# Packing the edge messages of a graph layer by 128-edge blocks with a slot table, in a four-layer graph network

## The reference

```python
xs = x[:, :C] @ (W_in2f_s / np.sqrt(C))
xv = jnp.einsum('nci,cf->nfi', x[:, C:].reshape(n, C, 3), W_in2f_v) / np.sqrt(C)
sj = xs[idx_j]; vj = xv[idx_j]
...
h = shifted_softplus(f_ij @ Wf1 + bf1)
W = (h @ Wf2 + bf2) * rcut_ij[:, None]
...                                      # products of sj, vj, a direction Yv and W: one message per edge
agg = jax.ops.segment_sum(x_ij, idx_i, num_segments=n)
```

## Time and profile before

| | |
|---|---|
| Time, median of 3 runs | 2368.18 us (2367.39 to 2369.47) |
| Time of the profiled execution | 2369.56 us |
| Its span (first to last instruction) | 2367.9 us |
| Fourth layer's edge loop | 1324 to 2318 us of the span |
| PE busy | 2152.2 us (91%), 8194 matmul instructions |
| DVE busy | 1680.3 us (71%) |
| ACT / POOL busy | 1208.7 us (51%) / 1285.7 us (54%) |

### The profile page before, as it was taken

The page is one execution under the profiler, slowest core; times in us unless marked ns, Lnnn a source line. Parts: engine busy times, 40 slices in busy tenths (PEclk is TensorE's granted clock), DMA queues, the critical chain, the costliest instruction groups (busy, mean ns, idle before and its releaser), DMA issues.

```text
span 2367.9 us, 39830 instructions
## 1 busy us (share of the span) xinstructions
PE 2152.2 (91%) x8194; PEld 1246.1 (53%) x8194; DVE 1680.3 (71%) x4797; ACT 1208.7 (51%) x3485; POOL 1285.7 (54%) x1637
## 2 busy tenths in 40 slices
PE   3798976777779999999999899999999999999997
PEld 3444434666664555454444555555555555555555
DVE  7998798888882431102225688888888888888885
ACT  0486566777770000000101667667676767666764
POOL 1578856666666666560002566666666666666650
PEclk9698987666669999999999899999999999999998
DMA  5200031111012111210000433333333333333331
GB/s 192 72 3 3 3 106 16 14 15 15 14 15 61 33 37 15 50 19 1 23 19 5 127 94 101 97 99 98 99 99 99 99 95 102 95 103 94 101 94 44
DMA packets 72826, 146.45 MB, mean 62 GB/s; under 512 B 23565, under 2 KB 36098, under 8 KB 72391
## 3 DMA queue, kind: packets, MB, share of 16 engines
q0 software_dynamic: 46080, 103.42, 17.9%
q1 hardware_dynamic: 23740, 36.99, 4.7%
q10 hardware_dynamic: 2946, 5.28, 0.6%
HBM read 122.80 MB, written 22.30 MB: 61 GB/s over the span
## 4 chain that ended last, share of the span: by engine, by line
PE 76%; DVE 17%; issue 4%; DVEq 2%; DMA 1%; ACT 0%; POOL 0%; ACTq 0%; SPq 0%; POOLq 0%
PE ps L840 26%; PE ps L589 11%; PE ps L608 8%; PE ps L826 4%; PE ps L781 4%; PE ps L828 3%; PE ps L827 3%; PE ps L829 3%; PE ps L739 3%; PE ps L681 3%; DVE dense L1332 2%; DVE adj_t L1356 2%; DVE dense L1331 2%; DVE adj_t L1161 2%; PE ps L704 1%
## 5 line engine op out<-in xcount | busy, mean ns | idle before, releaser
L840 PE MATMUL ps<-adj_t 128*128 128x512 f32 x1408 | 671.4, 599 | 0.0
L484 POOL DMA_INDIRECT src_table<-st_rec,st_idx x320 | 386.5, 1208 | 271.7 <-DMA st_rec<-records 179.5
L1048 ACT ACTIVATE adj_t<-adj_t 128x128 f32<-128x128 f32 x1056 | 344.6, 389 | 218.5 <-DVE adj_t L1510 217.4
L531 POOL DMA_INDIRECT adj_t<-z_table,adj_t x352 | 339.1, 963 | 168.4 <-DVE adj_t L1520 79.8
L840 PEld LDWEIGHTS ps<-adj_t 128*128 128x128 f32 x1408 | 253.3, 189 | 256.6 <-issue 216.3
L472 POOL DMA_INDIRECT pair_table<-dense x160 | 197.7, 1236 | 112.7 <-issue 112.7
L739 PE MATMUL ps<-dense 128*128 128x128 f32 x832 | 243.0, 429 | 0.0
L826 PE MATMUL ps<-dense_r 128*128 128x512 f32 x352 | 217.7, 618 | 2.3 <-POOL dense_r L539 2.3
L608 PE MATMUL ps<-wring,dense 128*128 128x512 f32 (+1 forms) x480 | 208.6, 597 | 4.6 <-issue 3.2
L739 PEld LDWEIGHTS ps<-dense 128*128 128x128 f32 x832 | 200.5, 296 | 15.6
L539 POOL TENSOR_TENSOR dense_r<-adj_t,dense_r 128x512 fp32r<-128x512 f32 x88 | 113.6, 1291 | 169.0 <-ACT dense_r L1057 168.8
(11 more groups left out here) (248 smaller groups left out, 3787.1 us busy)
## 6 DMA issues: line engine op xcount, KB each, us to landing
src_table<-dense SPq DMA_DIRECT2D x8, 704.0 KB, 7.0
adj_t<-src_table SPq DMA_DIRECT2D x88, 64.0 KB, 1.8
adj_t<-z_table,adj_t POOLq DMA_INDIRECT x352, 3.5
src_table<-st_rec,st_idx POOLq DMA_INDIRECT x320, 2.6
records<-dense SPq DMA_DIRECT2D x1, 5000.0 KB
st_rec<-records POOLq DMA_DIRECT2D x80, 62.5 KB, 2.2
wring<-in_edge_attr SPq DMA_DIRECT2D x2, 1562.5 KB
wring<-in_l_w SPq DMA_DIRECT2D x3, 1024.0 KB, 7.5
```

The source lines that it names most:

```text
L484: g.indirect_dma_start(out=src_table, out_offset=bass.IndirectOffsetOnAxis(ap=st_idx[0:EP, k, c:c + 1].bitcast(u32), axis=0), in_=st_rec[0 ...
L531: g.indirect_dma_start(out=zg[:, s, c, :], out_offset=None, in_=z_table, in_offset=bass.IndirectOffsetOnAxis(ap=dsti[:, s, c:c + 1].bitcas ...
L840: last = mm(bank[6 + h], oh[:, c, :], msg[:, c, h * D:(h + 1) * D], start=c == 0, stop=c == GROUP - 1)
L1048: last = A(msg[:, c, (2 + k) * P:(3 + k) * P], msg[:, c, MSG:MSG + P], ACT.Copy, scale=side[:, s, c, C_Y - ATT + k:C_Y - ATT + k + 1])
```

## The change

Tiles are padded to whole chunks (128 edges) instead of whole groups. At most `USED` = 322 chunks are then used. A tile's chunks are dealt out as items of four, two or one chunks, and a tile can have at most one item of two and one of one. Fixed places are kept for the worst case: 73 items of four (`FOURS`), 10 of two, 10 of one. A group now holds one item of four, or two items of two, or four items of one, so there are 73 + 5 + 3 = 81 groups (the last has two chunks), together 322 chunks. Items that a tile does not need load an empty chunk of padding.

Where an item's chunks begin in `src_table` and which tile it sums into is computed on the chip: `item_table` (DVE, some 50 small operations, behind the row sums of the adjacency), two small matmuls on PE (a new stage `slots`, between `deg` and `l1a_agg`), and two copies on DVE into `src_at` and `src_offs`. `chunk_steps(SRC)` and `chunk_places(SRC)` of the preparation go.

SP loads an offset from `src_at` into a register before each load, and issues one load per item (one, two or four per group). Each item has its own accumulation on PE and its own `add_sums` on DVE. In groups of twos and ones (`alone`), the filters of the next group stand ahead of scatters 2 and 3 instead of behind them. The loop now runs over groups 2 to 69; groups 0, 1 and 70 to 80 are written out.

```diff
-QUANT_LOG2 = [7, 9]
-GROUPS = (E + NT * (GROUP * P - 1)) // (GROUP * P)
-GROUPS += GROUPS % 2
-SRC_CHUNKS = GROUPS * GROUP
+USED = (E + NT * (P - 1)) // P
+FOURS = math.ceil((USED - 3 * NT) / 4)
+LISTS = [(4, FOURS, 0), (2, NT, 80), (1, NT, 96)]
+EMPTY = USED
+SRC_CHUNKS = 8 * math.ceil((EMPTY + GROUP) / 8)
+GROUPS = FOURS + NT // 2 + math.ceil(NT / GROUP)
+def items_of(g):
+    if g < FOURS:
+        return [(g, 0, 4)]
+    if g < FOURS + NT // 2:
+        return [(LISTS[1][2] + 2 * (g - FOURS) + k, 2 * k, 2) for k in range(2)]
+    one = GROUP * (g - FOURS - NT // 2)
+    return [(LISTS[2][2] + one + k, k, 1) for k in range(min(GROUP, NT - one))]
+LOOP_TO = (FOURS - 2) // 2
...
-                sp_eng.dma_start(recg[:, s, :, :].rearrange("p c w -> p (c w)"),
-                                 tsrc[:, ds(g * (GROUP * SRC_COLS), GROUP * SRC_COLS)]).then_inc(rec_in[s], 16)
+                for slot, c, n in items_of(g) if isinstance(g, int) else [(g, 0, GROUP)]:
+                    at = sp_eng.value_load(src_at[0:1, ds(slot, 1)], min_val=0, max_val=EMPTY * SRC_COLS)
+                    sp_eng.dma_start(recg[:, s, c:c + n, :].rearrange("p c w -> p (c w)"),
+                                     tsrc[:, ds(at, n * SRC_COLS)]).then_inc(rec_in[s], 16)
...
+            b = bank_for("slots", 0)
+            pe.wait_ge(slots_ready, 1)
+            for k in range(2):
+                last = mm(b[0:1, k * P:(k + 1) * P], slots[:, k:k + 1], ident[:, :], start=True, stop=True)
...
-                if c == 0 and not (isinstance(i, int) and gi == 0):
-                    pe.wait_ge(agg_added, gi)
+                if c == c0 and not (isinstance(i, int) and gi == 0):
+                    pe.wait_ge(agg_added, items_before(gi) + k)
...
-                scatter(i, s, 2)
-                if one:
-                    filter_out(*nxt, 0)
-                scatter(i, s, 3)
-                if one:
-                    filter_out(*nxt, 1)
+                for c in range(2, count):
+                    if one and alone:
+                        filter_out(*nxt, c - 2)
+                    scatter(i, s, c)
+                    if one and not alone:
+                        filter_out(*nxt, c - 2)
...
+            def item_table():
+                for k, (size, count, at) in enumerate(LISTS):
+                    link(v.tensor_copy(left_i, left))
...
+                v.tensor_reduce(slots[:, 1:2], place_of, AX.X, ALU.add).then_inc(slots_ready, 1)
...
+                for c in range(chunks_of(g)):
+                    one_hot(i, s, c)
+                    messages(i, s, c, nxt=(i if s == 0 else i + 1, 1 - s) if c == 1 and not tail else None)
+                    if c == 0 and not head:
+                        add_sums(g - 1, len(items_of(g - 1)) - 1 if isinstance(g, int) else 0)
+                    if c in ends:
+                        add_sums(g, ends[c])
```

More of the change, by code:

```diff
@@ L45 @@
 BURST = 8
-FILL = 44
+FILL = SRC_CHUNKS // 8
 assert SRC_CHUNKS % FILL == 0
@@ L261, in build @@
         pos_read = [sem(f"pos_read{s}") for s in range(2)]
-        off_done = [sem(f"off_done{s}") for s in range(2)]
+        off_done = sem("off_done")
         rows_ready = [sem(f"rows_ready{s}") for s in range(2)]
-        offs_ready = [sem(f"offs_ready{s}") for s in range(2)]
+        offs_ready = sem("offs_ready")
+        slots_ready = sem("slots_ready")
         tick = sem("tick")
@@ L423, in _ @@
             sp_eng.wait_ge(full, first["l2_agg"] + NT)
+            sp_eng.wait_ge(done["slots"], 1)
             load_group(0, 0)
             load_group(0, 1)
-            with sp_eng.Fori(1, L3_IT) as i:
+            with sp_eng.Fori(1, LOOP_TO + 1) as i:
                 load_group(i, 0)
                 load_group(i, 1)
+            for g in range(2 * LOOP_TO + 2, GROUPS):
+                load_group(g // 2, g % 2)
         @block.gpsimd
@@ L546, in group @@
                 if one:
+                    count = chunks_of(2 * i + s + 1)
                     gather(*nxt, 0)
@@ L561, in _ @@
             group(0, 1)
-            with pool.Fori(1, L3_IT - 1) as i:
+            with pool.Fori(1, LOOP_TO) as i:
                 group(i, 0)
                 group(i, 1)
-            group(L3_IT - 1, 0, two=False)
-            group(L3_IT - 1, 1, one=False, two=False)
+            for k in range(2 * LOOP_TO, GROUPS):
+                group(k // 2, k % 2, one=k + 1 < GROUPS, two=k + 2 < GROUPS)
         @block.tensor
@@ L836, in scatter @@
                 pe.wait_ge(oh_ready, n + 1)
-                if c == 0 and not (isinstance(i, int) and gi == 0):
-                    pe.wait_ge(agg_added, gi)
+                items = items_of(gi) if isinstance(gi, int) else [(gi, 0, GROUP)]
+                k = [q for q, (_, c0, count) in enumerate(items) if c0 <= c < c0 + count][0]
+                _, c0, count = items[k]
+                if c == c0 and not (isinstance(i, int) and gi == 0):
+                    pe.wait_ge(agg_added, items_before(gi) + k)
                 for h in range(2):
-                    last = mm(bank[6 + h], oh[:, c, :], msg[:, c, h * D:(h + 1) * D], start=c == 0, stop=c == GROUP - 1)
+                    last = mm(bank[6 + h], oh[:, c, :], msg[:, c, h * D:(h + 1) * D], start=c == c0, stop=c == c0 + count - 1)
                 last.then_inc(scat_chunk, 1)
@@ L845, in group @@
                 nxt = (i, 1) if s == 0 else (i + 1, 0)
-                filter_out(i, s, 2)
+                count = chunks_of(2 * i + s)
+                alone = isinstance(i, int) and 2 * i + s >= FOURS
+                if count > 2:
+                    filter_out(i, s, 2)
                 scatter(i, s, 0)
@@ L869, in _ @@
             group(0, 1)
-            with pe.Fori(1, L3_IT - 1) as i:
+            with pe.Fori(1, LOOP_TO) as i:
                 group(i, 0)
                 group(i, 1)
-            group(L3_IT - 1, 0, two=False)
-            group(L3_IT - 1, 1, one=False, two=False)
-            pe.wait_ge(agg_added, GROUPS)
+            for g in range(2 * LOOP_TO, GROUPS):
+                group(g // 2, g % 2, one=g + 1 < GROUPS, two=g + 2 < GROUPS)
+            pe.wait_ge(agg_added, items_before(GROUPS))
             tbank = [(bank[0], bank[1]), (bank[4], bank[5])]
@@ L1083, in group @@
                     first_vy(*nxt, 0)
-                c_part(i, s, 3)
+                if count > 3:
+                    c_part(i, s, 3)
                 if two:
@@ L1099, in _ @@
             group(0, 1)
-            with act.Fori(1, L3_IT - 1) as i:
+            with act.Fori(1, LOOP_TO) as i:
                 group(i, 0)
                 group(i, 1)
-            group(L3_IT - 1, 0, two=False)
-            group(L3_IT - 1, 1, one=False, two=False)
+            for g in range(2 * LOOP_TO, GROUPS):
+                group(g // 2, g % 2, one=g + 1 < GROUPS, two=g + 2 < GROUPS)
             def sums(t):
@@ L1411, in _ @@
             dve.wait_ge(tiles_summed, 1)
+            item_table()
             dve.wait_ge(full, first["l0_agg"] + 12)
@@ L1422, in _ @@
             dve.wait_ge(done["deg"], 3)
+            b = taken("slots", 0)
+            link(v.tensor_scalar(src_at, b[0:1, 0:P], float(EMPTY * SRC_COLS), None, ALU.add))
+            v.tensor_copy(src_offs, b[0:1, P:2 * P]).then_inc(done["slots"], 1)
             scaled_T("l1a_agg")
@@ L1544, in _ @@
             group(0, 1)
-            with dve.Fori(1, L3_IT - 1) as i:
+            with dve.Fori(1, LOOP_TO) as i:
                 group(i, 0)
                 group(i, 1)
-            group(L3_IT - 1, 0)
-            group(L3_IT - 1, 1, tail=True)
-            add_sums(L3_IT - 1, 1)
+            for g in range(2 * LOOP_TO, GROUPS):
+                group(g // 2, g % 2, tail=g + 1 == GROUPS)
+            add_sums(GROUPS - 1, len(items_of(GROUPS - 1)) - 1)
             def activated(t):
```

129 lines of the change are left out of this document (82 added, 47 removed).

## The result

| | before | after |
|---|---|---|
| Time, median | 2367.82 us (4 runs, 2367.39 to 2369.47) | 2296.62 us (4 runs, 2295.20 to 2300.43) |
| Ratio to before | | 0.9702, 95% interval 0.9690 to 0.9713 |
| Profiled execution / its span | 2369.56 / 2367.9 us | 2297.48 / 2295.8 us |
| First `add_sums` / last | 1334.77 / 2316.75 us | 1331.15 / 2244.61 us |
| Between them | 981.98 us | 913.46 us |

The change makes the kernel 3% faster, 71.2 us between the medians. Between the two profiles 68.5 us of it lie between the first and the last `add_sums`, and 3.6 ahead of the first.

The account below looks back on a forecast made before the run. PE was taken to bound the loop. The tail's 167.3 us become 100.8, with 0.3 more saved 66.8 us less: 2369.6 to 2302.8, predicted median 2302 us, 80% range 2296 to 2310.

Parts of the forecast that it names:

- What bounds the loop, and the count: Fourth layer's edge loop: PE bounds it at 11.24 us a group; 322 chunks instead of 352, old groups 73 to 87 take 167.3 us.
- Written-out groups 70 to 72: Loop's end: these groups, now written out, take 11.19 us instead of 11.31, 0.3 us less.
- The groups of twos: Tail: PE waits 0.65 us inside a group and 0.87 at its end, 12.8 us for each of five groups.
- The groups of singles: Tail: three rounds of 3.59 us and one of 4.0 with `hidden`, 14.8 us for each of two groups.
- The last group: End of the tail: two rounds with no `hidden`, 7.2 us.
- SP's lookup: Loop and tail: SP's register load, once per group of the loop, is hidden in 6.2 us of slack and counts nothing.
- rival 4: Loop: SP's lookup beyond about 6 us costs up to one microsecond per group for each; chance 0.02, plus 0.02 for a part.
- The table and the small matmuls: Ahead of the loop: `item_table`'s 11 us hide in DVE's 73.4 us wait; with the matmuls net zero, within 1 us.
- rival 1: Whole kernel: the forecast, round trips as reckoned, 2302 us, within 2297 to 2308; chance 0.80.
- the upper bound: Tail: every boundary costs one more wake-up of about 0.25 us; 20 boundaries, 5 us more.
- Rival 2, the clock: Tail: PE's clock falls in the singles only, 2321 us, chance 0.07; in the twos too, 2369 us, chance 0.03.
- Rival 3, DVE alone counts: Tail: boundaries cost PE nothing, only DVE's work counts; 89.2 us, 11.6 less, 2291 us in all; chance 0.06.

Follow-up runs that it names:

- 88 fours: The changed kernel with 88 groups of four chunks and no items of two or one, leftover chunks not summed: 2367.49 us, ratio 0.9993.
- 20 more lookups: The changed kernel with 20 extra register loads on SP before each load of a group of four: 2742.64 us, ratio 1.1332.
- fours alone: The changed kernel with 88 or 81 groups of four and no items of two or one: 2367.49 us and 2284.62 us.
- early load: The changed kernel with DVE's register load right after an add instead of right before the next, in written-out groups: 2295.43 us, ratio 0.9694.
- both edits: The changed kernel with DVE's register load right after an add and, in the twos, two filters at every boundary: 2290.19 us, ratio 0.9669.
- second session: One of three sessions of runs; the kernel before takes 2421.9 us in it, 2368.9 in the first and third.
- old order of filters: The changed kernel with the next group's filters behind scatters 1, 2 and 3 in the written-out groups too: ratio 0.9701.

## Why the prediction was right, point by point

- **What bounds the loop, and the count.** Right. The loop's period stayed at 11.30, and with 88 groups under the new table the time is that of before. The prediction had 167.3 us for the old groups 73 to 87, and the kernel of 88 fours has 167.5 there (2147.58 to 2315.07).
- **Written-out groups 70 to 72.** 0.3 us were predicted; groups 69 to 72 lost 0.3, all of groups 0 to 72 together 1.3. The extra 1.0 is spread over the loop, 0.015 us a group, and is in each kernel with 93 items (11.295 to 11.299 a group; the one with 20 more lookups aside) but in neither with fours alone (11.313). The prediction had it at nothing; what makes it was not tried.
- **The groups of twos.** 12.8 predicted, 12.50 measured. The mechanism is right and the round trip was mis-sized: 1.46 + 2.13 were put for it, 1.37 + 2.01 were measured. The two halves were taken from different groups: behind the first add PE was still busy with filters, and the second add had DVE's register load ahead of it. So the two boundaries add 1.26 us to the 11.24 of a group of fours, not 0.65 + 0.87. (The brackets' 0.35 and 0.57 are another measure: they count from the modelled end of the matmul before.) That is 1.4 us in the five groups.
- **The groups of singles.** 14.8 predicted, 15.2 measured, for another reason than the one given. The prediction let PE's round trip of 3.59 set three rounds of four, with DVE's load at 0.6 behind line 1520's start and so just hidden. In the run it is 0.80 from that row to the add, PE's round trip is shorter, and DVE's chain of add, chunk and load sets every round (3.64, 4.24). The early load shows it: 14.0 a group, with PE's round trip at 3.45. The two errors, PE's round 0.2 too long and DVE's 0.2 too short, nearly cancel in the sum.
- **The last group.** 7.2 predicted, 7.1 measured. The eight groups: 100.8 and 100.07.
- **SP's lookup.** Right, it is hidden, with 6.1 us to spare. The prediction had 6.2 us ahead of a lookup of 0.5, though its own numbers (8.5 less 0.33 and 1.8) make 6.4, so 5.9 behind it. A lookup is 0.59 us of SP, and above the margin each microsecond came through whole (11.7 less 6.1 of the changed kernel's rows are the 5.6 measured), as rival 4 priced it at its worst. Its condition wasn't met.
- **The table and the small matmuls.** The table's 11 us went into DVE's wait, as predicted. The stretch ahead of the loop was put at zero within 1 us, and the sign that went with it did not come: PE's first scatter stands at 1321.38 us instead of 1324.85. The profiles' first adds differ by 3.6, of which 2.6 stand at a row ahead of every edited one on DVE and PE. What is left, 1.0 earlier, is at the edge of the predicted band and inside the spread of the table above; whether the change gains there stays open.
- **Sum.** For the profiled execution 2302.8 us were predicted, 2297.5 measured, 5.3 less: 1.0 from the loop's period, 0.7 from the tail, 3.6 from the start of the loop (against zero). The largest part is the one that differs from run to run. For the median, 2302 stand against 2296.6, at the very edge of the stated 2296 to 2310 and just under the 2297 of rival 1. The second execution of the same kernel gave 2298.2, so on which side of such an edge a median falls is in part luck. Of the upper bound, the 0.25 us of a wake-up stand in none of the prediction's rows, and no run shows one by itself.
- **Rival 2, the clock.** It held 1.00 through twos and singles. The rule of the Trainium skill that was weighed there (TensorE: Matmul & The Clock Gate, "HAM oscillation — how this bites in real kernels") didn't make these groups throttle: pauses of 0.35 to 1.69 us in every round, PE busy 72% of the singles' window, and no fall. Longer pauses weren't tried.
- **Rival 3, DVE alone counts.** Half true in a way that the prediction didn't see: DVE counts in the singles, but with its register load on the chain, which makes them dearer and not cheaper. With the load out of the way and two filters at each boundary the tail is 92.6 us, near the 89.2 that the prediction took as the lower bound.

## What to carry to other kernels

Cutting padding to a finer unit pays by the count of units and costs at each new boundary; here 30 units of 2.8 us were saved for 12 boundaries of 1.4 us. Price a boundary as a loop of two engines: scatter to add, add to scatter, and ask for each half which engine's queue is really later, the one that the trace names or one that is loading a register. Where an engine loads a register for an operation that closes such a round, the load belongs right behind the operation of the round before, not right ahead of its own; and two small edits on two engines that take turns being late are worth more together (7.4) than their sum (4.0). Work that PE does between two scatters of one item lengthens that item's chain, while the same work at a boundary is hidden in the round trip: with both edits the filters of the twos stand at the boundaries alone, and a group takes 11.42 us instead of 12.50.

## What the runs showed of the hardware that was not expected

- A register load on DVE's queue delays the next vector operation by 0.5 to 0.6 us (0.80 against 0.29 and 0.82 against 0.21 us from the last message row to the add), and on SP a lookup takes 0.59 us in sequence, though the load itself has 0.27 and its register steps 0.15. On DVE the trace books this time as a wait for PE in 91 of 93 adds.
- The start of the loop moves by 4.2 us (1331.09 to 1335.29) between five executions whose instructions ahead of it are the same. Part of what lies between before and after is where PE's granted clock goes from 0.50 to 1.00: from 96 to 100 us it is 0.50 in before and 0.59 in after, from 100 to 104 us 0.60 and 1.00. Windows of PE alone, busy us (matmuls), clock, DMA share, GB/s, of before and of after, where both run the same instructions:

```profile
100.00:105.00 5.00, 5.00 (x24) 0.68 0.08 2
```

```profile
100.00:105.00 5.00, 5.00 (x36) 1.00 0.08 2
```

  PE is busy in both, and in the second the clock has risen earlier, for 12 matmuls more in 5 us.
- In the second session the loop started 42 to 59 us later and ran at the same speed; DVE's line 1214 starts at 244 to 259 us there instead of 203 to 208. In the run with the old order of filters PE's clock is as in the changed kernel at first (105 to 130 us: 1.00, 130 to 160: 0.99), yet PE does 252 matmuls in these 55 us instead of 335; from 160 to 200 us the clock is lower too (0.88 against 1.00). The instructions themselves last no longer (DVE's line 1263 has 570 ns in both), but from 105 to 200 us ACT stands idle for 15.5 us and PE, ahead of line 690, for 6.7 us with nothing but "issue" as the cause, which the changed kernel's profile doesn't have there. What makes it is open.
